# First feed-forward layer: one block normalized on GpSimd, second root and shared products reordered; token weights and the lines' bias moved

## The chip, the cores and the metric

The kernel runs on one core of a Trainium2 chip. The metric is the time of one execution on the device in microseconds (us); where several executions were timed, their median counts.

## The reference

`x` is (2, 2048, 256) in float32. Three layers follow one another, each added to `x`:

```python
x = x + 0.5 * ffn(layernorm(x))
x = x + attention(layernorm(x))      # causal, 16 heads, queries and keys are normalized line coordinates
x = x + 0.5 * ffn(layernorm(x))

def ffn(x):                          # 4096 tokens, 16 experts, each token goes to 2 of them
    scores = softmax(x @ gate_w.T)   # + gate_b; the 2 best of 4 groups, then the 2 best experts
    y = sum over the 2 experts of weight * (silu(x @ We1 + be1) * (x @ We3 + be3)) @ We2 + be2
    z = silu(x @ ws1 + bs1) * (x @ ws3 + bs3) @ ws2 + bs2      # shared experts, 256 wide
    return y + z
```

## The kernel before

Tokens stand in 32 tiles of 128, in 8 blocks of 4 tiles. Each engine has its own program, written out by hand; the order of the work is the order of the code, and semaphores are all that joins the engines. The change touches the first feed-forward layer (`ffn`) and the stage behind it (`lines`), which adds the experts' rows to `x` and makes queries, keys and values.

**The front of `ffn`, from 0 to about 36 us.** VectorE takes the statistics of the blocks as they arrive, and sums them up in two halves (blocks 0 to 3, blocks 4 to 7). For each half ScalarE takes the root (`take_root`, L572) and VectorE inverts it (L695). Then the blocks are normalized into `stage` (`normalize`: VectorE at L701 makes blocks 0 and 4 to 7, ScalarE at L588 blocks 1 to 3). TensorE turns each block (L451, 8 transposes into two of four banks, so that block n waits for the copies of block n - 2), and the turned blocks are copied to `xnt` (`keep_tiles`: ScalarE at L557 for blocks 0 to 5, VectorE at L707 for 6 and 7). Between them TensorE multiplies products nobody reads (`keep_busy`, L440). From each half of `xnt` come the logits (`logits_of`, L428), which ScalarE copies (`keep_logits`, L561) and TensorE turns back (`turn_logits`, L435). VectorE's `softmax` (L778 to L792) subtracts the maximum, waits for ScalarE's exponential (`take_exp`, L577; its table is loaded at the `hint` of L609) and finds the group scores.

**The middle, to about 103 us.** TensorE makes six shared up products (`shared_up`, L472) and down products (`shared_down`, L485), each in turn, and between them the small products of the routing. VectorE works through the routing, multiplies (`multiply`, L735) and adds (`add_shared`, L743). The last routing product is the inversion (L512), which waits for ScalarE's scaled marks (L582); from it VectorE makes `token_of` (L899), by which GpSimd gathers the rows of each expert tile (`bring`, L668). Behind `token_of` VectorE adds the last shared product and then computes the token weights (`weigh`, L828 to L830), which only the lines stage reads.

**The expert loop, to about 231 us**, has 79 turns: TensorE turns gathered rows (L525), multiplies up (L536) one turn later and down (L547) three turns later. ScalarE copies the up weights (L636) and the turned rows (L641) and gates (L648). VectorE copies the down weights (L914), multiplies (L927, `prod_done`) and adds the bias (L921). An up product waits for the `prod_done` of two turns before, since it shares two banks.

**The lines stage, to about 373 us.** For each block GpSimd gathers the experts' rows (L1363), VectorE adds them to `x` (`add_rows`, L1632), takes statistics (L190), subtracts (L1681 to L1684), and splits lines (`split_lines`, L1690 to L1705); ScalarE normalizes (L233), copies points and values (L1535, L1537) and stores features (L1525); TensorE turns the block (L1419), turns features (L1438) and projects (L1453 to L1456). Two shared products of `ffn` are left over for this stage; the last is added by `add_shared(1)` (L1593) at VectorE's step 2, and when that is done TensorE multiplies a bias (`project_bias`, L1403), which VectorE adds (L1628) at the end of its step 2.

The attention (to about 873 us) and the second feed-forward layer follow.

## Time and profile before

| | |
|---|---|
| runs | 1141.83, 1141.98 and 1144.21 us, median 1141.98 |
| profiled execution | 1139.9 us, of which the trace spans 1137.9 |
| mean granted clock of TensorE | 0.988 of full speed |
| busy, share of the span | TensorE 90%, ScalarE 76%, VectorE 58%, GpSimd 40% |

The profile's views used here: the timeline lists each engine's instructions by start, with the length, the operation (output <- input), how many are merged in the row, and in brackets the idle time before them and what ended it. The windows give each engine's busy time in a stretch and TensorE's granted clock there (1.00 is 2.4 GHz, 0.50 is 1.2 GHz). Starts of instructions that follow on their engine can lie before the end of the one before them, since they overlap by some 0.1 us.

### The profile page before, as it was taken

The numbers are of one execution on the slowest core, as the hardware profiler recorded it, in microseconds if no ns is written. First come the engines' busy times: TensorE is split into PE (matmuls) and PEld (weight loads), VectorE is DVE, ScalarE is ACT, GpSimd is POOL, SyncE is SP. The second block draws the span as 40 slices with busy tenths as digits, with TensorE's granted clock in tenths as the row PEclk, the third lists the DMA queues.
The fourth block names the chain that finished last, engine by engine and source line by source line (L and its number), as shares of the span: only waits on it lengthen the run. The fifth ranks groups of instructions, "written<-read, shape, count | busy, mean of one in ns | idle before, by whom it ended". The sixth has DMA issues, their size and how long they took to land.

```text
span 1137.9 us, 23905 instructions
## 1 busy us (share of the span) xinstructions
PE 1028.8 (90%) x7549; PEld 559.1 (49%) x7549; DVE 664.2 (58%) x1477; ACT 870.4 (76%) x1245; POOL 460.0 (40%) x671
## 2 busy tenths in 40 slices
PE   8998999989887788989899898989899999999995
PEld 4456999946554122222122222222223578999843
DVE  6898788768997422332134345356548686445655
ACT  4226777745887999999999999999998237777710
POOL 1003666457730424331221323431313345677755
PEclk9999999999999899999999999999999999999998
DMA  8911555545766221020201022120100965566655
GB/s 291 276 58 48 172 162 173 155 128 162 223 211 196 73 72 56 11 61 10 66 11 41 30 71 79 29 76 20 48 1 21 282 190 157 166 190 188 182 162 153
DMA packets 125717, 133.80 MB, mean 118 GB/s; under 512 B 13224, under 2 KB 111888, under 8 KB 125616
## 3 DMA queue, kind: packets, MB, share of 16 engines
q1 hardware_dynamic: 109056, 90.95, 25.2%
q0 software_dynamic: 14448, 39.47, 12.9%
q10 hardware_dynamic: 2112, 2.10, 0.6%
q8 instruction: 56, 0.92, 0.3%
q14 instruction: 45, 0.37, 0.1%
HBM read 80.43 MB, written 52.04 MB: 116 GB/s over the span
## 4 chain that ended last, share of the span: by engine, by line
PE 31%; ACT 24%; issue 14%; DVE 8%; POOL 2%; DVEq 1%; DMA 1%; ACTq 0%; POOLq 0%
ACT wide L2077 22%; PE banks L1961 6%; PE banks L2452 6%; PE banks L2377 5%; PE banks L2466 3%; PE banks L1935 2%; PE banks L2386 2%; PE banks L2440 1%; DVE x_res L1632 1%; POOL wide L2083 1%; PE banks L1453 1%; DVE wide L1681 1%; PE banks L1456 1%; PE banks L1975 1%; DVE attn_lines_parts L190 1%
## 5 line engine op out<-in xcount | busy, mean ns | idle before, releaser
L2077 ACT ACTIVATE wide<-banks 128x1536 f32<-128x1536 f32 (+1 forms) x384 | 491.7, 1479 | 5.4 <-PE banks L1935 3.8
L1961 PE MATMUL banks<-wide,attn_attend_v_now 128*32 128x512 f32 (+3 forms) x2560 | 287.7, 540 | 1.7 <-POOL wide L2083 1.6
L2083 POOL TENSOR_SCALAR_AFFINE_SELECT wide<-wide 128x256 f32<-128x256 f32 (+1 forms) x320 | 118.2, 398 | 382.8 <-ACT wide L2077 379.1
L1935 PE MATMUL banks<-attn_attend_q_now,attn_attend_k_now 32*128 32x512 f16 (+3 forms) x1280 | 150.5, 354 | 57.4 <-ACT wide L2077 54.3
L1935 PEld LDWEIGHTS banks<-attn_attend_q_now,attn_attend_k_now 32*128 32x128 f16 x1280 | 38.7, 91 | 291.9 <-ACT wide L2077 246.9
L668 POOL DMA_INDIRECT f_region<-xn_rows,f_token_of x79 | 78.3, 991 | 125.1 <-DVE f_token_of L899 82.4
L2128 DVE COPY sums<-banks 128x512 f32<-128x512 f32 x32 | 22.1, 691 | 163.3 <-PE banks L1961 163.3
L2452 PE MATMUL banks<-f_xnt 128*128 128x128 f32 x752 | 100.5, 277 | 3.8 <-DVE f_more L2678 2.9
L2452 PEld LDWEIGHTS banks<-f_xnt 128*128 128x128 f32 x752 | 91.3, 191 | 6.7 <-issue 5.8
L2565 POOL DMA_INDIRECT last_rows_in<-xn_rows,f_spare x72 | 68.8, 956 | 62.1 <-DVE f_stage L2626 24.4
L1961 PEld LDWEIGHTS banks<-wide,attn_attend_v_now 128*32 128x32 f32 x2560 | 56.3, 108 | 73.7 <-issue 71.8
L536 PE MATMUL banks<-f_region,wide 128*128 128x128 f32 x632 | 84.4, 277 | 0.6 <-DVE wide L927 0.6
L2535 ACT ACTIVATE f_xnt<-last_w_all 128x514 f32 x94 | 59.5, 632 | 33.1 <-issue 24.2
L2670 DVE TENSOR_TENSOR f_xnt<-banks,last_w_all 128x256 f32<-128x256 f32 x94 | 39.9, 425 | 65.9 <-PE banks L2466 54.7
L536 PEld LDWEIGHTS banks<-f_region,wide 128*128 128x128 f32 x632 | 76.7, 191 | 2.4 <-issue 1.3
L636 ACT ACTIVATE wide<-f_w_all 128x514 f32 x79 | 50.0, 632 | 30.9 <-issue 30.4
L2156 DVE TENSOR_TENSOR x_res<-banks,x_res 128x512 f32<-128x512 f32 x30 | 20.7, 691 | 89.6 <-PE banks L1975 89.6
L2466 PE MATMUL banks<-last_w_all,f_more 128*128 x188 | 58.1, 391 | 1.5 <-DVE f_more L2678 1.5
L914 DVE COPY wide<-f_w_all 128x512 f32 x79 | 38.8, 491 | 19.8 <-issue 19.1
L547 PE MATMUL banks<-wide 128*128 128x256 f32 x158 | 47.1, 381 | 0.4 <-DVE wide L927 0.4
L2549 ACT ACTIVATE f_xnt<-banks,f_xnt 128x128 f32<-128x128 f32 x94 | 34.5, 367 | 10.6 <-PE banks L2452 9.4
L1363 POOL DMA_INDIRECT f_region<-y_slots,attn_lines_rows_of x32 | 37.8, 1183 | 11.8 <-issue 8.5
(370 smaller groups left out, 1765.2 us busy)
## 6 DMA issues: line engine op xcount, KB each, us to landing
y_half<-f_xnt SPq DMA_DIRECT2D x94, 128.0 KB
y_slots<-wide SPq DMA_DIRECT2D x79, 128.0 KB, 1.7
attn_v<-f_more SPq DMA_DIRECT2D x32, 256.0 KB, 3.0
attn_attend_v_now<-attn_v SPq DMA_DIRECT2D x32, 256.0 KB, 3.2
x_res<-L_attn_x SPq DMA_DIRECT2D x8, 512.0 KB, 7.5
xn_rows<-f_w_all SPq DMA_DIRECT2D x8, 512.0 KB, 5.1
attn_q<-attn_lines_q_out SPq DMA_DIRECT2D x8, 512.0 KB, 3.4
attn_k<-attn_lines_k_out SPq DMA_DIRECT2D x8, 512.0 KB, 4.1
```

Source lines behind the costliest of these rows:

```text
L536: last = pe.matmul(bank[2 + m][:, f * P:(f + 1) * P], w_up[:, at, col_at:col_at + INTER], rows_t[:, m, c * P:(c + 1) * P], start=(c == 0), ...
L636: act.activation(w_up[:, j, :], w_all[:, bass.ds(expert, 1), 0:UP].rearrange("p o f -> p (o f)"), ACT.Copy).then_inc(sem.up_kept, 1)
L668: pool.indirect_dma_start(out=rows_in[:, n % ROUND, :], out_offset=None, in_=xn_rows, in_offset=bass.IndirectOffsetOnAxis(ap=token_of[:, n ...
L1935: last = pe.matmul(score[i % SLOTS][:, j, column:column + columns(u)], k_now[rows, kt * P:(kt + 1) * P], q_now[rows, qc * QW + c0:(qc + 1) ...
L1961: last = pe.matmul(out_bank[qc][rows, c0:QW], v_now[:, kt, rows], probs[:, place, column:column + columns(u)], start=(kt == 0), stop=(u == ...
L2077: act.activation(probs_flat[:, at:at + width_of[i]], score_flat[i % SLOTS][:, 0:width_of[i]], ACT.Exp, scale=SCALE).then_inc(sem.exp_done, 1)
L2083: pool.affine_select(out=part, in_=part, compare_op=ALU.is_ge, fill=0.0, base=0, pattern=[[0, part.shape[1]], [1, P]], channel_multiplier= ...
L2377: last = pe.matmul(bank[f][:, :], ws13[:, c, f * P:(f + 1) * P], xnt_of(i)[:, c, :], start=(c == 0), stop=(c == DC - 1))
L2452: last = pe.matmul(bank[2 + m][:, f * P:(f + 1) * P], w_up[:, at, col_at:col_at + INTER], rows_t[:, m, c * P:(c + 1) * P], start=(c == 0), ...
L2466: pe.matmul(bank[4 + m][:, 0:D], prod_t[:, at, :], w_all[:, bass.ds(expert, 1), UP:UP + D].rearrange("p o f -> p (o f)"), start=True, stop ...
L2535: act.activation(w_up[:, n % ROUND, :], w_all[:, bass.ds(expert, 1), 0:UP].rearrange("p o f -> p (o f)"), ACT.Copy).then_inc(sem.up_kept, 1)
L2565: pool.indirect_dma_start(out=rows_in(n), out_offset=None, in_=xn_rows, in_offset=bass.IndirectOffsetOnAxis(ap=s.token_of[:, place_of_turn ...
```

## The change

Five edits, all in the order of the code.

1. Front: GpSimd normalizes block 3 (`POOL_BLOCK`), which ScalarE did. ScalarE takes the second root ahead of `keep_tiles(1)`. ScalarE keeps the turned blocks 0 to 4, 6 and 7, VectorE only 5.
2. Front: the first logits come after TensorE has turned block 4, not 5, and are turned back after block 5, not 6. ScalarE's table hint comes before the first `keep_logits`, and the first exponential between the copies of blocks 6 and 7. VectorE's `softmax` is cut in `shift` and the rest. TensorE's filler matmuls are 48 and 10, where they were 42, 4 and 4.
3. The token weights are computed in two parts, one ahead of each of the last two sums (`weigh_pick`, `add_half`), on a semaphore of their own.
4. In the expert loop, turn 1 alone: the up product of tile 0 goes ahead of the turning of tile 1's rows.
5. In the lines stage `add_shared(1)` goes ahead of the second pair of sums of VectorE's step 2, and `project_bias` ahead of block 1's projection on TensorE.

```diff
-        ACT_BLOCKS, DVE_TURNED = (1, 2, 3), (BLOCKS - 2, BLOCKS - 1)
+        ACT_BLOCKS, POOL_BLOCK, DVE_BLOCKS = (1, 2), 3, (0, 4, 5, 6, 7)
+        ACT_TURNED, DVE_TURNED = (0, 1, 2, 3, 4, 6, 7), 5
...
+            elif n == POOL_BLOCK:
+                eng.wait_ge(sem.pool_staged, 1)
             else:
-                eng.wait_ge(sem.staged, sum(m not in ACT_BLOCKS for m in range(n)) + 1)
+                eng.wait_ge(sem.staged, DVE_BLOCKS.index(n) + 1)
+
+        def wait_turned_kept(eng, n):
+
+            if n == DVE_TURNED:
+                eng.wait_ge(sem.dve_xnt_ready, DC)
+            else:
+                eng.wait_ge(sem.xnt_ready, DC * (ACT_TURNED.index(n) + 1))
...
-            keep_busy(42)
+            keep_busy(48)
...
-                    pe.wait_ge(sem.xnt_ready, DC * (n - 1))
+                    wait_turned_kept(pe, n - 2)
...
-                if n in (1, 2):
-                    keep_busy(4)
-                if n == HALF + 1:
+                if n == 1:
+                    keep_busy(10)
+                if n == HALF:
                     pe.wait_ge(sem.gate_ready, 1)
                     logits_of(0)
-                if n == HALF + 2:
+                if n == HALF + 1:
                     turn_logits(0)
...
+                second = isinstance(n, int) and n == 1
+                if runs(n, 0) and not second:
+                    turn(n, j, r)
...
+                if second:
+                    turn(n, j, r)
...
             keep_tiles(0)
             normalize(2)
-            keep_tiles(1)
             take_root(1)
-            normalize(3)
-            keep_tiles(2)
-            keep_tiles(3)
-            keep_tiles(4)
-            keep_tiles(5)
+            for n in (1, 2, 3, 4):
+                keep_tiles(n)
+            act.activation(hint[:], s.root[:, 0:1], ACT.Exp)
             keep_logits(0)
-            act.activation(hint[:], s.root[:, 0:1], ACT.Exp)
+            keep_tiles(6)
             take_exp(0)
+            keep_tiles(7)
             keep_logits(1)
             take_exp(1)
...
+            pool.wait_ge(sem.rstd_ready, 1)
+            for t in range(POOL_BLOCK * BT, (POOL_BLOCK + 1) * BT):
+                last = pool.tensor_scalar(stage[:, POOL_BLOCK, t % BT, :], x[:, t, :], s.mean[:, t:t + 1], s.rstd[:, t:t + 1],
+                                          ALU.subtract, ALU.mult)
+            last.then_inc(sem.pool_staged, 1)
...
-            for i in DVE_TURNED:
-                keep_tiles(i)
+            keep_tiles(DVE_TURNED)
...
+            shift(0)
             softmax(0)
+            shift(1)
             softmax(1)
...
+            def weigh_pick(k, pick):
+                dve.tensor_tensor(work, pick, probs, ALU.mult).then_inc(sem.weighed, 1)
+                dve.wait_ge(sem.weighed, 2 * k + 1)
+                dve.tensor_reduce(weight[:, k, :], by_expert(work), AX, ALU.add).then_inc(sem.weighed, 1)
+                dve.wait_ge(sem.weighed, 2 * k + 2)
+
+            def halve_weights():
                 step(dve.tensor_scalar(weight[:].rearrange("p k t -> p (k t)"), weight[:].rearrange("p k t -> p (k t)"), 0.5, None, ALU.mult))
...
-            add_shared(5)
-            weigh()
+            weigh_pick(0, first)
+            add_half(5, 0)
+            weigh_pick(1, second)
+            add_half(5, 1)
+            halve_weights()
...
                 last.then_inc(sem.turned, 1)
+                if isinstance(n, int) and n == 1:
+                    project_bias()
             if has_block(n, 2):
...
                     pe.matmul(bank[2 + j], now(1), w_now[:, 1, :], start=False, stop=True).then_inc(sem.projected, 1)
                 if isinstance(n, int) and n == 0:
                     shared_down(1)
-                if isinstance(n, int) and n == 1:
-                    project_bias()
...
                 combine_pair(n, q, r, 0)
                 if n == 2:
                     measure_lines(n - 1, q)
+                    add_shared(1)
                 stats.sum_up(dve, n, q, combine_pair(n, q, r, 1))
...
-                if isinstance(n, int) and n == 2:
-                    add_shared(1)
```

In the copies of blocks (`wide<-banks`) the output is `xnt`; `f_w_all` holds `stage`; `f_region` at the exponential holds the logits. ScalarE in the front, from the copy of block 0, before:

```order
L557 ACTIVATE wide<-banks 128x512 x2
L588 ACTIVATE f_w_all<-x_res,f_gap,f_rstd 128x256 x4
L557 ACTIVATE wide<-banks 128x512 x2
L572 ACTIVATE f_root<-f_var 128x16
L588 ACTIVATE f_w_all<-x_res,f_gap,f_rstd 128x256 x4
L557 ACTIVATE wide<-banks 128x512 x8
L561 ACTIVATE f_logits_t<-banks 128x512
L609 ACT_TABLE_LOAD
L609 ACTIVATE f_hint<-f_root 128x1
L577 ACTIVATE f_region<-f_region 128x256
L561 ACTIVATE f_logits_t<-banks 128x512
```

and with the change:

```order
L573 ACTIVATE wide<-banks 128x512 x2
L604 ACTIVATE f_w_all<-x_res,f_gap,f_rstd 128x256 x4
L588 ACTIVATE f_root<-f_var 128x16
L573 ACTIVATE wide<-banks 128x512 x8
L620 ACT_TABLE_LOAD
L620 ACTIVATE f_hint<-f_root 128x1
L577 ACTIVATE f_logits_t<-banks 128x512
L573 ACTIVATE wide<-banks 128x512 x2
L593 ACTIVATE f_region<-f_region 128x256
L573 ACTIVATE wide<-banks 128x512 x2
L577 ACTIVATE f_logits_t<-banks 128x512
```

The second root (`f_root`) stands one copy sooner, four normalizations are gone, the table is loaded before the first copy of logits, and two more copies of blocks stand around the first exponential.

VectorE from `token_of` (`f_token_of`) to the first copy of down weights, before:

```order
L899 TENSOR_TENSOR f_token_of<-f_token_f,f_empty_f 128x80
L743 SCALAR_TENSOR_TENSOR x_res<-banks,x_res 128x512 x2
L828 TENSOR_TENSOR f_region<-f_region 128x512
L829 TENSOR_REDUCE weight<-f_region 128x32
L828 TENSOR_TENSOR f_region<-f_region 128x512
L829 TENSOR_REDUCE weight<-f_region 128x32
L830 TENSOR_SCALAR weight<-weight 128x64
L911 TENSOR_LOAD f_expert_of
L911 ISA x2
L914 ISA
L914 COPY wide<-f_w_all 128x512
```

and with the change:

```order
L927 TENSOR_TENSOR f_token_of<-f_token_f,f_empty_f 128x80
L852 TENSOR_TENSOR f_region<-f_region 128x512
L854 TENSOR_REDUCE weight<-f_region 128x32
L760 SCALAR_TENSOR_TENSOR x_res<-banks,x_res 128x512
L852 TENSOR_TENSOR f_region<-f_region 128x512
L854 TENSOR_REDUCE weight<-f_region 128x32
L760 SCALAR_TENSOR_TENSOR x_res<-banks,x_res 128x512
L858 TENSOR_SCALAR weight<-weight 128x64
L942 TENSOR_LOAD f_expert_of
L942 ISA x2
L945 ISA
L945 COPY wide<-f_w_all 128x512
```

The two sums (`x_res<-banks,x_res`) stood together ahead of the weights; each now has a product and a reduction ahead of it, and one small instruction is left behind them.

TensorE in the lines stage, before, from the last tile of block 1's projection to the turning of features (`f_xnt`):

```order
L1453 MATMUL banks<-attn_lines_w_now,attn_lines_xt 128x512
L1455 MATMUL banks<-attn_lines_w_prev,attn_lines_xt 128x128 x2
L1456 MATMUL banks<-attn_lines_w_now,attn_lines_xt 128x512
L1403 MATMUL banks<-attn_lines_w_o,attn_lines_b_v_wide 128x256 x2
L1419 MATMUL banks<-ident,f_stage 128x128 x8
L1438 MATMUL banks<-ident,f_xnt 128x128 x32
```

and with the change, from the last shared down product (`wide,heads`) to the first tile of block 1's projection:

```order
L1425 MATMUL banks<-wide,heads 128x256 x8
L1450 MATMUL banks<-ident,f_stage 128x128 x8
L1434 MATMUL banks<-attn_lines_w_o,attn_lines_b_v_wide 128x256 x2
L1486 MATMUL banks<-attn_lines_w_now,attn_lines_xt 128x512
L1488 MATMUL banks<-attn_lines_w_prev,attn_lines_xt 128x128 x2
L1489 MATMUL banks<-attn_lines_w_now,attn_lines_xt 128x512
```

The bias product (`b_v_wide`) stood behind the projection and ahead of the turning of block 2; it now stands between the turning of block 1 and block 1's projection.

## Rows read from the trace of the kernel before

**Rows 1.** windows: us from:to, length, PE, PEld, DVE, ACT, POOL busy, PEclk, DMA
```profile
36.00:97.00 61.00, 60.60 (x227) 35.11 (x225) 56.37 (x85) 25.17 (x76) 0.00 (x0) 1.00 0.45 136
113.00:228.00 115.00, 114.93 (x881) 106.13 (x880) 90.89 (x228) 86.93 (x220) 68.43 (x70) 1.00 0.55 166
280.00:352.00 72.00, 61.66 (x367) 40.01 (x365) 68.60 (x161) 60.51 (x120) 36.67 (x34) 0.95 0.68 207
```

**Rows 2.** timeline of TensorE: second logit product, first shared up product
```profile
32.58 1.92 PE L428 MATMUL banks<-wide,f_gate_t 128*32 128x512 f32 x16 [1.47 <-DVE wide L707]
...
35.71 1.88 PE L472 MATMUL banks<-wide 128*128 128x512 f32 x4
```

**Rows 3.** timeline of ScalarE in the front (start us, length, operation, idle before)
```profile
20.30 1.10 ACT L557 ACTIVATE wide<-banks 128x512 f32<-128x512 f32 x2
21.25 0.25 ACT L572 ACTIVATE f_root<-f_var 128x16 f32<-128x16 f32 x1
...
28.84 0.60 ACT L561 ACTIVATE f_logits_t<-banks 128x512 f32<-128x512 f32 x1 [0.80 <-PE banks L428]
29.46 1.28 ACT L609 ACT_TABLE_LOAD   x1
```

**Rows 4.** timeline of VectorE in the front
```profile
21.53 0.25 DVE L695 RECIPROCAL f_rstd<-f_root 128x16 f32<-128x16 f32 x1 [1.75 <-ACT f_root L572]
21.82 5.26 DVE L701 TENSOR_SCALAR f_w_all<-x_res,f_mean,f_rstd 128x256 f32<-128x256 f32 x16
29.84 2.60 DVE L707 COPY wide<-banks 128x512 f32<-128x512 f32 x4 [2.76 <-PE banks L451]
```

**Rows 5.** timeline of TensorE at the start of the expert loop
```profile
107.44 0.44 PE L525 MATMUL banks<-ident,f_region 128*128 128x128 f32 x2
108.44 1.13 PE L536 MATMUL banks<-f_region,wide 128*128 128x128 f32 x8 [0.56 <-DVE wide L927]
```

**Rows 6.** timelines of VectorE, ScalarE and GpSimd at the same place
```profile
105.59 0.20 DVE L830 TENSOR_SCALAR weight<-weight 128x64 f32<-128x64 f32 x1
106.84 0.43 DVE L914 COPY wide<-f_w_all 128x512 f32 x1 [1.06 <-issue]
105.99 0.37 ACT L648 ACTIVATE f_region<-banks,wide 128x128 f32<-128x128 f32 x1 [0.49 <-PE banks L536]
...
107.16 0.37 ACT L641 ACTIVATE f_region<-banks 128x256 f32<-128x256 f32 x1
104.51 1.14 POOL L668 DMA_INDIRECT f_region<-xn_rows,f_token_of  x1 [0.31 <-issue]
```

**Rows 7.** timeline of VectorE in the lines stage
```profile
269.66 1.40 DVE L1632 SCALAR_TENSOR_TENSOR x_res<-f_region,weight,x_res 128x256 f32<-128x256 f32 x3 [1.32 <-DMA f_region<-y_slots,slots]
...
273.65 1.28 DVE L1593 SCALAR_TENSOR_TENSOR x_res<-banks,x_res 128x512 f32<-128x512 f32 x2
...
279.90 0.42 DVE L1628 TENSOR_TENSOR attn_lines_b_o<-banks,attn_lines_b_o 128x256 f32<-128x256 f32 x1 [0.71 <-PE banks L1403]
```

**Rows 8.** timeline of TensorE in the lines stage
```profile
270.07 1.12 PE L1453 MATMUL banks<-attn_lines_w_now,attn_lines_xt 128*128 128x512 f32 x2 [1.51 <-ACT attn_lines_xt L1515]
...
278.83 1.03 PE L1403 MATMUL banks<-attn_lines_w_o,attn_lines_b_v_wide 128*128 128x256 f32 x4
```

**Rows 9.** timeline of GpSimd, its one elementwise instruction in the front
```profile
17.57 0.41 POOL L662 TENSOR_SCALAR f_bs<-f_bs 128x256 f32<-128x256 f32 x1
```

**Rows 10.** timeline of TensorE: first turning, and filler matmuls in that stretch
```profile
15.01 1.06 PE L451 MATMUL banks<-ident,f_w_all 128*128 128x128 f32 x8 [1.34 <-DVE f_w_all L701]
...
18.43 1.91 PE L440 MATMUL banks<-ones 128*128 128x512 bf16 x4
```

**Rows 11.** windows again, one stretch of the front
```profile
17.50:20.70 3.20, 3.07 (x11) 1.53 (x10) 2.18 (x11) 3.20 (x8) 0.48 (x2) 0.50 0.98 344
```

**Rows 12.** source line L668, GpSimd's row gathers: min/median/max ns
```profile
L668 POOL DMA_INDIRECT f_region<-xn_rows,f_token_of x79: 940/947/1298, 100.4 to 220.4; - x79
```

**Rows 13.** timeline of ScalarE in the lines stage
```profile
286.77 0.84 ACT L1549 ACTIVATE wide<-attn_lines_line 128x768 f32<-128x768 f32 x1 [0.65 <-DVE attn_lines_line L1684]
```

42 lines of the change are left out of this document (21 added, 21 removed).

## The prediction

> **What bounds the kernel now.** I read the busy times by stage first, then the timeline of each engine at the places that the change touches. From 36 to 97 us TensorE works 60.60 of 61 us, and in the expert loop, from 113 to 228 us, 114.93 of 115; in the lines stage from 280 to 352 us it is VectorE, 68.60 of 72 [rows 1]. So time can only be won ahead of these stretches, where TensorE or VectorE get to their unbroken work late, and each microsecond won there moves all that follows, since the later order is fixed.
>
> There are three such places. In the front, TensorE waits 1.47 us before the second logits, which start at 32.58, and starts the shared products at 35.71 [rows 2]; ahead of them ScalarE takes the second root at 21.25, behind a copy that began at 20.30 [rows 3], VectorE waits 1.75 us for that root, and its copies of the last two blocks wait until 29.84 [rows 4]. At the end of the middle part the inversion waits for ScalarE's marks; nothing in the change shortens that chain, which starts behind VectorE's `multiply` and so moves with TensorE's products. At the start of the loop the third up product (108.44) waits for VectorE [rows 5], which is busy with token weights to 105.79 and first copies at 106.84 [rows 6]. In the lines stage VectorE adds a shared product at 273.65, on its own path, and waits 0.71 us for the bias product [rows 7], which TensorE makes at 278.83 [rows 8].
>
> **The front: 1.4 us won.** The root moves from 21.25 to 20.30 (the place of the copy), so its reciprocal and VectorE's 16 normalizations come 0.95 us sooner; they take 5.26 us [rows 4] and end at 26.13 where it was 27.08. ScalarE loses one block of normalizations. From 20.4 it copies blocks 1 to 4 at 1.10 us each [rows 3]. Each turning needs some 1.1 us and waits for the copy of two blocks before, and block 4 is staged by 22.2, so I put the end of the four copies at 25.0. The table load of 1.28 us and the hint's 0.2 then end at 26.5. The first logits (1.92 us, as the second [rows 2]) can start at 23.8, when block 3 is kept, and are done before that; their copy of 0.60 us [rows 3] ends at 27.1, and TensorE turns them (0.6) to 27.7 and block 6 to 28.6. ScalarE copies block 6 to 29.7, takes the exponential (0.4) to 30.1, and copies block 7 to 31.15. VectorE's copy of block 5 (two of the four in 2.60 us [rows 4]) ends by 28.2 and its `shift` by 29.0, ahead of the exponential. So the second logits start at 31.15 where it was 32.58: 1.43 us sooner, and from there to the first shared product the order is what it was. VectorE's routing gets more than 2 us ahead by the cut `softmax`, but its first `multiply` reads the third and fourth up product, so it falls back to TensorE's lead. I take 1.4 us.
>
> What carries this: GpSimd must have block 3 staged by 21.6, when TensorE gets to it. It waits only for the first reciprocal, at 13.4. An instruction of its kind and width took 0.41 us [rows 9], four of them 1.6 us. At twice that they would still be done at 16.7, so this costs nothing on TensorE's path, and the iotas and the halving behind them, which nobody needs before 78 us, are only some 0.1 us later than they were. The store of block 3 on SP's queue stands behind block 2's and now finds it ready. The stores and the loads of experts' weights move up with the normalizations; they were landed 30 us before the loop.
>
> The fillers: six more of 0.21 us end at 14.95, just ahead of the first turning at 15.01, and cover the 1.34 us that TensorE idled there [rows 10]. From 17.5 to 20.7 the granted clock was 0.50, which is 1.2 GHz [rows 11], after TensorE had idled these 1.34 us and, behind the first turning, 0.6 for a load. I take it that with the 1.34 filled the clock stays at 2.4 GHz. Then the ten fillers take 2.1 us from 18.1 and end before block 2 is staged (20.4).
>
> **The start of the loop: 0.85 us won.** The weights are four instructions of 0.72 us and one of 0.2. Two go in the wait for the first sum, of which 0.86 us was idle, and two in the wait for the second, 1.03 us. VectorE is through at 104.0 where it was 105.79, both without the front's lead. Its copies then begin at 105.05 (1.06 us of issue [rows 6]). ScalarE's first gate comes at 105.99 [rows 6]. With turn 1 reordered the first up product starts at 104.4 instead of 104.9, and the row copy of tile 1 is later by as much, so the gate stays near 106.05. The first `prod_done` is then at 106.8 (it was 108.3), and the third up product is held by the turning at 107.44 [rows 5] and by ScalarE's row copy of 107.16 to 107.53 [rows 6]. It starts at 107.65, 0.8 us sooner. The row of the next tile was issued 1.44 us after the gather of 104.51 [rows 6], which landed 2.9 us after its issue (its turning is the one of 107.44), so it is there by 108.9, where TensorE turned it at 109.84. From then TensorE has no gap. I take 0.85; bounds: 0 (if rows land a gather's time later) and 1.0.
>
> At this place the Trainium skill speaks against the change (SBUF — State Buffer, section "SBUF: two separate sides"): a VectorE copy from SBUF to SBUF in its fast mode locks GpSimd out of writing gather descriptors, and VectorE's copies now lie over more of the first gathers. By it the win would be some 0.5, if a gather is late by the most that one exceeded the median by. The trace has 79 gathers at 0.947 us in the median and 1.298 at most [rows 12], nearly all beside such copies. So the sum keeps 0.85.
>
> **The lines stage: 1.5 us won.** `add_shared(1)` is 1.28 us [rows 7] and moves into a place where VectorE waited 1.32 us for gathered rows (269.66), so it is nearly free there; the splitting of lines starts 1.0 us sooner, since the size's root then ends it, not the sum. The bias product is done long before, so the 0.71 us are gone too: 1.7 us at VectorE. Against it: TensorE's bias product, 0.86 us to the next start, waits for the sum to end at 269.2, so the projection starts at 270.1 to 270.35 where it was 270.07 [rows 8]. Behind it ScalarE's copies and features would end at 286.2 to 286.5, and its squares, which waited 0.65 us for VectorE [rows 13], now start then, while VectorE wants them at 287.1. That takes back 0.1 to 0.3 us. Queries behind this wait on TensorE are the block's projection and all turnings, which is why it counts. GpSimd's gathers are not moved by it and keep 4 us of lead over the sums. I take 1.5; bounds 0.9 and 1.7.
>
> Everything else is moved without a cost: two semaphores more are cleared at the end of the layer, of some fifty.
>
> **Sum.** 1.4 + 0.85 + 1.5 = 3.75 us. The profiled execution took 1139.9 us, so the like of it would take 1136.15. The runs shown have a median of 1141.98, 2.1 us above it; the forecast is for such a median, 1138.2 us, 0.33% faster. A measurement of this kernel tells some 0.2% (2.3 us) from no change, so the forecast stands only 1.5 us beyond that.
>
> **Rivals.**
>
> *The clock falls all the same.* If TensorE runs at 1.2 GHz from 17.5, the ten fillers are slow: four took 1.91 us there [rows 10]. Ten reach to about 21.7, block 2 is turned 1.2 us late, and the front's 1.4 is 0.2. Or it falls before the second logits: TensorE then idles from 29.4 to 31.15 behind turnings alone, and a stretch of 3.2 us at half speed costs 1.6. Either way the win is 2.2 to 2.5, and the time 1139.6. For it: it fell once in the trace behind less idleness than 2 us. Against it: it did not fall behind the 1.47 us [rows 2]. 20%.
>
> *GpSimd holds VectorE up.* By the same section of the skill GpSimd and some VectorE instructions exclude one another for a whole instruction. As a mechanism of this kernel: the four normalizations on GpSimd, 1.6 us at 0.41 [rows 9], lie beside VectorE's of block 0 and its statistics. Should VectorE stop for them, the second root is 1.15 us late again, the win is 2.6, and the time 1139.4. Against it: GpSimd's instruction [rows 9] ran beside statistics that took no longer for it. 7%.
>
> *Won places are taken by what is next.* The loop's first rows land when they did relative to their turnings (loop 0), or ScalarE sets the lines stage (0.9), or both: 2.3 us won, 1139.7. 14%.
>
> *Slower.* A low clock that lasts. TensorE is without a gap from 35.7, so half of each microsecond at 0.50 there is lost. The trace's stretch of 3.2 us [rows 11] costs 1.6. From 7.5 us of it on, the 3.75 are used up; ten would give 1.25 us slower, with a measurement's scatter 1143 to 1145. Nothing in the trace shows one so long; 3%.
>
> **Numbers.** The forecast gets 56%. Faster by over 0.2% holds most of it and about half of the first three rivals, less what scatter takes: 0.64. Within 0.2%: 0.32. Slower: 0.04. The range goes from 1135.4 (4.6 us won, if all bounds are high, and 2 of scatter) to 1141.2 (the rivals at 2.2, with 1.4 of scatter).
>
> **What would show it.** The second root near 20.3 and second logits near 31.2; granted clock 1.00 from 17.5 to 20.7; the first shared product at 34.3, and token rows asked for at 99.0; VectorE's first down copy at 103.6 where it was 106.84, and turnings without a gap from the fifth, 2.25 us sooner than before; in the lines stage VectorE without a wait behind its step 2, and the first exponential of the attention at 370.9 where it was 374.6. Wrong would be: a granted clock of 0.50 anywhere from 17 to 36 us, a shared product that starts behind 35, or a gap of ScalarE or TensorE behind block 1's projection that VectorE waits for.

## The result, and the profile after

The changed kernel takes 1139.9 us in the median of 12 runs (1137.84 to 1142.43), the kernel before 1142.52 us in the median of 12 beside it (1141.33 to 1145.58). The ratio is 0.9974, with a 95% interval of 0.9963 to 0.9985: 0.26% or 3.0 us faster, where 3.75 us were forecast. The profiled execution of the changed kernel spans 1138.2 us, 0.3 us *more* than the one shown of the kernel before. So one execution hides what the medians show, and the first question is why. Among the runs of all kernels below, one took 3473.52 us (edit 5 alone); the median given there counts it, the ratio leaves it out.

The windows of the changed kernel, answering to [rows 1] and [rows 11]:

```profile
core 0: us, PE busy (x) PEld busy (x) DVE busy (x) ACT busy (x) POOL busy (x), PEclk, DMA share, GB/s
36.00:97.00 61.00, 59.76 (x240) 35.20 (x240) 56.18 (x85) 25.40 (x78) 0.00 (x0) 1.00 0.42 127
113.00:228.00 115.00, 115.00 (x880) 106.21 (x878) 90.37 (x228) 86.42 (x219) 67.72 (x69) 1.00 0.54 164
280.00:352.00 72.00, 60.15 (x375) 39.15 (x376) 68.36 (x159) 62.40 (x124) 34.66 (x32) 0.98 0.69 212
17.50:20.70 3.20, 2.99 (x18) 1.57 (x17) 2.71 (x13) 3.20 (x8) 2.23 (x6) 1.00 0.96 333
102.90:104.70 1.80, 1.78 (x8) 1.80 (x9) 0.85 (x2) 0.63 (x1) 1.43 (x2) 0.50 0.33 87
104.70:106.00 1.30, 1.16 (x7) 0.79 (x5) 0.00 (x0) 0.57 (x2) 0.84 (x2) 0.50 0.39 107
...
366.00:369.00 3.00, 3.00 (x31) 3.00 (x29) 1.16 (x2) 2.13 (x3) 0.00 (x0) 0.50 1.08 316
```

The same engines fill the same stretches. What differs is the clock column. The front's low stretch is gone (1.00 from 17.5 to 20.7, where [rows 11] have 0.50), and low stretches stand at the start of the expert loop and at the end of the lines stage. The kernel before has two of its own in the lines stage, from 297 to 301 and from 325 to 328 us (hence its 0.95 in the window from 280), the changed kernel one from 308 to 311.

**The front** came as forecast. TensorE's timeline in the changed kernel, and GpSimd's:

```profile
18.14 2.12 PE L450 MATMUL banks<-ones 128*128 128x512 bf16 x9
20.43 3.42 PE L461 MATMUL banks<-ident,f_w_all 128*128 128x128 f32 x24 [0.16 <-ACT f_w_all L604]
...
31.01 1.92 PE L438 MATMUL banks<-wide,f_gate_t 128*32 128x512 f32 x16 [1.58 <-ACT wide L573]
...
34.14 2.31 PE L482 MATMUL banks<-wide 128*128 128x512 f32 x5
```

```profile
13.45 5.04 POOL L671 TENSOR_SCALAR f_w_all<-x_res,f_mean,f_rstd 128x256 f32<-128x256 f32 x4 [9.33 <-DVE f_rstd L714]
...
19.33 0.40 POOL L681 TENSOR_SCALAR f_bs<-f_bs 128x256 f32<-128x256 f32 x1
```

The first shared product starts at 34.14 where [rows 2] have 35.71: 1.57 us won. GpSimd's four normalizations took 5.04 us, not 1.6.

**The start of the loop** gave nothing in this execution:

```profile
101.95 0.41 PE L534 MATMUL banks<-ident,f_region 128*128 128x128 f32 x2 [1.46 <-DMA f_region<-xn_rows,f_token_of]
102.92 2.04 PE L550 MATMUL banks<-f_region,wide 128*128 128x128 f32 x8 [0.57 <-ACT f_region L655]
104.76 1.06 PE L534 MATMUL banks<-ident,f_region 128*128 128x128 f32 x4
105.96 1.29 PE L550 MATMUL banks<-f_region,wide 128*128 128x128 f32 x8
107.08 0.38 PE L534 MATMUL banks<-ident,f_region 128*128 128x128 f32 x2
107.30 1.06 PE L550 MATMUL banks<-f_region,wide 128*128 128x128 f32 x8
108.19 0.60 PE L563 MATMUL banks<-wide 128*128 128x256 f32 x2
```

Rows were asked for 1.57 us sooner, and VectorE made its first down copy at 103.20 where [rows 6] have 106.84. But the first up product's eight matmuls take 2.04 us, not 1.06: TensorE runs at 1.2 GHz. The lead was 1.56 us at the inversion and is 1.21 at the loop's steady turnings (108.63, was 109.84).

**The lines stage** gave 1.34 us, and lost 2.0 at its end. VectorE in the changed kernel:

```profile
267.10 1.28 DVE L1624 SCALAR_TENSOR_TENSOR x_res<-banks,x_res 128x512 f32<-128x512 f32 x2
268.30 1.79 DVE L1662 SCALAR_TENSOR_TENSOR x_res<-f_region,weight,x_res 128x256 f32<-128x256 f32 x4
...
272.85 0.23 DVE L1720 TENSOR_SCALAR attn_lines_size<-attn_lines_size 128x128 f32<-128x128 f32 x1
...
356.80 0.95 DVE L1648 TENSOR_REDUCE attn_lines_size<-wide 128x128 f32<-128x768 f32 x1 [4.01 <-ACT wide L1580]
...
363.98 2.23 DVE L1711 TENSOR_TENSOR wide<-f_spare 128x768 f32<-128x768 f32 x3 [1.50 <-ACT f_spare L1566]
```

The four sums at 268.30 have no wait ahead of them, where [rows 7] have 1.32 us, and the splitting of lines starts at 272.85, 2.0 us sooner. VectorE led the kernel before by 1.29 us at the stage's start, by 2.63 at block 3's size (L1648, 286.16; was 288.79), and by 2.61 at 356.80. Then TensorE's turnings of features ran at 1.2 GHz (351.20, 32 of them in 2.85 us where such 32 take 1.96 at 2.4 GHz), VectorE waited for ScalarE at 363.98, 1.22 us ahead of before, and the attention's first exponential started at 374.01, only 0.60 us sooner than before. How much of this is the clock's, the other profiles tell. From the reduction answering to 356.80 to the first exponential lie 15.19 or 15.20 us in all seven profiles (on chips like this one) without a low stretch between 352 and 358 us, the kernel before among them. With one it is 16.76 and 16.78 us in two kernels below, and 17.21 here, where a second stretch lies over the next 32 turnings too (365.74, 3.55 us). So a low stretch there costs 1.6 to 2.0 us. The rest went mostly in the second layer's expert loop (0.24 us ahead at its first product, 0.59 behind at its last); the length of that loop differs by 1.5 us among five executions at a granted clock of 1.00, so nothing in the change is needed for it.

Two theories follow. *A*: each place gives what its rows show, and the sum is 3.75 us. *B*: the places give that only while TensorE's clock is up. Low stretches of some 3 us come up once or more in the parts where TensorE idles, and when the front's is gone, one comes up where TensorE is needed.

### The profile page after: what moved, and what is told of

Its sections match the earlier page's. It is cut to its first block, busy times and chain, and to the rows that moved or that the text cites. A ratio compares the mean times of both kernels' runs of the same rounds, so it can differ in the third digit from the quotient of the medians.

```text
span 1138.2 us, 23920 instructions
## 1 busy us (share of the span) xinstructions
PE 1032.4 (91%) x7554; PEld 562.4 (49%) x7557; DVE 662.9 (58%) x1475; ACT 870.1 (76%) x1243; POOL 464.7 (41%) x675
## 4 chain that ended last, share of the span: by engine, by line
PE 30%; ACT 24%; issue 14%; DVE 7%; POOL 3%; DVEq 1%; DMA 1%; ACTq 0%; POOLq 0%
ACT wide L2107 22%; PE banks L1991 6%; PE banks L2482 6%; PE banks L2407 5%; PE banks L2496 3%; PE banks L1965 2%; PE banks L2416 2%; POOL f_region L1394 1%; PE banks L2470 1%; POOL wide L2113 1%; DVE x_res L1662 1%; DVE wide L1711 1%; PE banks L2005 1%; PE banks L1486 1%; DVEq L2696 1%
## 5 line engine op out<-in xcount | busy, mean ns | idle before, releaser
L2186 DVE TENSOR_TENSOR x_res<-banks,x_res 128x512 f32<-128x512 f32 x30 | 20.7, 691 | 89.6 <-PE banks L2005 89.5
```

## The experiments

They ran on several chips. On one, the kernel before itself took 1227.95 us; it is treated by itself. Ratios are always to the kernel before on the same chip, as they were recorded; they differ from the quotient of the two medians by up to 0.1%. "Behind the inversion" is the time from the inversion's end to the first down product: 10.89 us in the kernel before, 11.23 in the changed one.

### The edits apart, on the slower chip

```diff
# front alone: edits 1 and 2
+        ACT_BLOCKS, POOL_BLOCK, DVE_BLOCKS = (1, 2), 3, (0, 4, 5, 6, 7)
...
# loop alone: edits 3 and 4
+            weigh_pick(0, first)
+            add_half(5, 0)
...
+                if second:
+                    turn(n, j, r)
...
# lines alone: edit 5
+                    add_shared(1)
...
+                if isinstance(n, int) and n == 1:
+                    project_bias()
```

> The kernel before with the front's edits alone (1 and 2). Theory A (each place gives what its own rows show, and the places add up): the first shared up product starts 1.5 us sooner (34.2 us), nothing else changes its length, and the median is 1.5 us below the kernel before (ratio 0.9987). Theory B (TensorE's clock takes part of it back): the front still gives 1.5 us at its own end, but a stretch of 3 us at a granted clock of 0.50, which the kernel before had inside the front, now stands at another place where TensorE is needed, and the median is only 0.5 us or less below. Sign of it: the lead at the first steady turning of the expert loop is under 1.2 us.

> The kernel before with edits 3 and 4 alone (token weights between the last sums; first up product ahead of the second turning). Theory A (the edit frees VectorE, and the gates were its customers): the third up product and the steady turnings start 0.85 us sooner (109.0 us for the fifth turning, was 109.84), the granted clock stays 1.00 from 102 to 107 us since the front has taken its low stretch already, and the median falls by 0.8 us. Theory B (the order of the edit itself makes TensorE idle 1.46 and 0.57 us in a row, and the clock falls behind that): 0.50 from about 104 us, the first up product takes 2.0 us instead of 1.06, and the steady turnings come no sooner than before: gain 0 or a loss of 0.3 us. Theory C (ScalarE's gate and row copies bound it at any clock): clock 1.00 and gain under 0.3 us.

> The kernel before with edit 5 alone (the shared sum and the bias product sooner in the lines stage). Theory A: VectorE leads by 1.3 us from block 3 on (first normalization of block 3 at 288.8 where it was 290.12), and the attention's first exponential starts 1.3 us sooner (373.3, was 374.61); median 1.3 us lower. Theory B (a low clock of TensorE at the end of the stage takes it back): the lead of 1.3 us holds to 356 us and is gone at the first exponential if the granted clock is 0.50 in the last turnings of features, and stays if it is 1.00 there. Theory C (at the end of the stage ScalarE or TensorE bound, so that VectorE's lead is lost at any clock): lead under 0.5 us at the first exponential with a granted clock of 1.00 from 350 to 371.

> The changed kernel without its edits 3 and 4: front and lines alone. If the loop's edits gave 0.85 us under the changed kernel, this is 0.8 us slower than it, 2.1 us faster than the kernel before. If they gave nothing because the clock fell at the start of the loop (theory B), this is as fast as the changed kernel: 2.7 to 3.0 us faster than before (ratio 0.9975), and the lead at the fifth turning is 1.5 us, where the changed kernel had 1.21.

Measured: front 1226.82 us (ratio 0.9981, 0.9962 to 1.0), loop 1228.21 (1.0004, 0.9989 to 1.0019), lines 1230.62 (1.0022, 1.0005 to 1.004), front with lines 1230.28 (1.0023, 1.0007 to 1.0038). The intervals of the first two are too wide for their forecasts of 0.13% and 0.07%: the medians settle neither. Up to the loop the profiles can be read like the others. The first shared product was 1.5 to 1.7 us sooner in both kernels that have its edits (34.27 and 34.33; 35.85 and 35.99 in the two that have not). At the loop's start, with edits 3 and 4 alone:

```profile
103.57 0.41 PE L524 MATMUL banks<-ident,f_region 128*128 128x128 f32 x2 [1.37 <-DMA f_region<-xn_rows,f_token_of]
104.54 1.13 PE L540 MATMUL banks<-f_region,wide 128*128 128x128 f32 x8 [0.57 <-ACT f_region L647]
...
108.66 0.60 PE L553 MATMUL banks<-wide 128*128 128x256 f32 x2
```

The first down product comes 10.00 us behind the inversion, against 10.88 in the kernel with edit 5 alone, whose loop is that of before. So edits 3 and 4 give 0.88 us up to this product at full clock, and theory C of that run (ScalarE bounds it) falls. What becomes of it behind this product can't be read here: all four kernels on this chip have a further wait of 1.4 to 1.8 us ahead of an up product between 111 and 114 us, with the edits and without. Theory B of the same run has this execution against it: TensorE idled 1.37 and 0.57 us, and the clock stayed. In both kernels with the front's edits it fell between 102 and 108 us, though their loop is that of before (11.02 and 11.21 us behind the inversion). So the low stretch doesn't need the loop's edits; in these four profiles it goes with the front's. With the old loop it cost only 0.14 and 0.33 us there. The lead that theory B of the front's run wanted gone was 1.58 us at the fifth turning (108.54, against 110.12 in the kernel with edit 5 alone). Whether the loop's edits pay within the changed kernel, the question of the fourth run, stays unanswered here, since the changed kernel itself did not run on this chip.

The expectation for edit 5 was wrong here: a loss of 0.2%, not a gain. On this chip every engine stood for some 16 us early in the lines stage (ScalarE 16.37 to 16.72 us, up to 276 to 279 us), so the gathered rows had long landed, and the wait that was to hide the shared sum was not there. The wait for the bias product was there: 2.23 and 2.99 us of VectorE without edit 5, none with it. But with edit 5, alone or with the front's, ScalarE waited for transfers behind that, which it did not without:

```profile
310.58 1.02 ACT L1542 ACTIVATE attn_lines_q_out<-banks 128x1024 f16<-128x1024 f16 x1 [2.20 <-DMA x_res<-L_attn_x]
312.09 1.02 ACT L1542 ACTIVATE attn_lines_q_out<-banks 128x1024 f16<-128x1024 f16 x1 [0.48 <-DMA x_res<-L_attn_x]
314.28 1.02 ACT L1542 ACTIVATE attn_lines_k_out<-banks 128x1024 f16<-128x1024 f16 x1 [1.17 <-DMA x_res<-L_attn_x]
317.14 1.02 ACT L1542 ACTIVATE attn_lines_k_out<-banks 128x1024 f16<-128x1024 f16 x1 [1.84 <-DMA x_res<-L_attn_x]
```

VectorE's step from block 2's reduction to block 3's takes 21.56 us in both kernels with edit 5, against 17.93 and 18.51 in the two without: the gain at the bias product is more than lost. Why transfers land later there, and why only with edit 5, stays open. All runs below are from chips on which the kernel before takes 1143 to 1144 us.

### The changed kernel again

Nothing is edited.

> The changed kernel again, as it is, as the level for the two kernels with fillers and as a second profile. On a chip like the first: 1139.9 us, ratio 0.9974 to the kernel before, first down product 11.2 us behind the inversion with the granted clock at 0.50 around 103 to 106 us. Theory B (the fall at the loop's start is a consequence of the front's edits and comes every time) wants the low stretch again; if it is a matter of the single execution, the clock is 1.00 there in this one.

Measured: 1141.13 us, ratio 0.9966 (0.9951 to 0.9982), which is 3.9 us by the ratio and 2.8 by the medians. Its twelve runs fall into two groups, four from 1136.57 to 1137.79 and eight from 1140.07 to 1143.36 us. The mean granted clock doesn't tell the groups apart (0.984 and 0.985 are in both). The profiled run is one of the four. Windows, then TensorE:

```profile
102.00:104.00 2.00, 1.39 (x11) 1.21 (x12) 0.68 (x3) 1.02 (x2) 1.70 (x2) 1.00 0.41 125
104.00:106.00 2.00, 1.78 (x15) 1.43 (x14) 0.95 (x3) 1.52 (x4) 1.39 (x3) 1.00 0.25 72
252.00:255.00 3.00, 2.00 (x3) 0.97 (x4) 1.92 (x6) 0.95 (x2) 2.39 (x3) 0.57 0.39 108
255.00:258.00 3.00, 3.00 (x14) 2.04 (x13) 2.45 (x10) 0.66 (x2) 2.22 (x3) 0.86 0.36 111
```

```profile
102.05 0.41 PE L534 MATMUL banks<-ident,f_region 128*128 128x128 f32 x2 [1.44 <-DMA f_region<-xn_rows,f_token_of]
103.02 1.13 PE L550 MATMUL banks<-f_region,wide 128*128 128x128 f32 x8 [0.56 <-ACT f_region L655]
...
107.09 0.60 PE L563 MATMUL banks<-wide 128*128 128x256 f32 x2
```

With the same waits of 1.44 and 0.56 us, the clock stays at 2.4 GHz here, and the first down product comes at 107.09, 10.01 us behind the inversion. The same program, 1.22 us apart at this place: whether the clock falls here is a matter of the single execution. Nor is there a low stretch from 352 to 356 us, and the first exponential comes at 371.98, 2.03 us sooner than in the first profile; their spans are 2.2 us apart. One came at 252 us, which the first profile hasn't, where VectorE then waited 2.27 us for ScalarE's root. The Trainium skill (TensorE: Matmul & The Clock Gate, "Part 1: The HAM clock gate") says of the slow matmuls at a kernel's start that their count differs between executions of the same kernel; the two traces show the like in the middle of one (0.50 and 1.00 in the same place).

### Fillers at the loop's start, and in the lines stage

`fill(k)` multiplies k products of 128x512 in bf16 that nobody reads, into a bank that is free then.

```diff
# loop: both kernels
+            fill(6)
...
+                    if second:
+                        fill(2)
...
# lines: the second kernel only
+                if after(n, 3):
+                    pe.wait_ge(sem.q_ready, 2 * (n - 2))
+                    for _ in range(8):
+                        pe.matmul(bank[6][:, :], core.ones[:], core.ones[:, 0:1].to_broadcast([P, BW]), start=True, stop=True)
```

> The changed kernel with eight filler matmuls more at the start of the expert loop: six while TensorE waits for the first gathered rows, two between the first turning and the first up product; into a bank that nobody reads then. The edits 3 and 4 without the front's gave 0.88 us there (first down product 10.00 us behind the inversion's end, against 10.88 in the kernel before), at a granted clock of 1.00; with the front's edits the clock fell at this place in every profile so far, and the first down product came 11.23 us behind the inversion in the changed kernel. Theory B (the low stretch of 3.2 us moved from the front to the loop's start and takes the gain of edits 3 and 4): with fillers the granted clock is 1.00 from 100 to 108 us, the first down product comes 10.0 to 10.1 us behind the inversion, and this kernel is 1.0 to 1.2 us faster than the changed one on the same chip, if the low stretch does not then come up at another place that counts. Theory D (the clock falls here whatever TensorE does): 0.50 all the same, and fillers delay the first up product by up to 0.4 us: 0 to 0.4 us slower.

> As the kernel with fillers at the loop's start, and in the lines stage eight filler matmuls (1.7 us) in TensorE's wait of 2.2 to 2.7 us ahead of each turning of features from block 1's on. Theory B: in the changed kernel VectorE's lead of 2.6 us over the kernel before fell to 0.6 us in the last 15 us of the stage, where the granted clock was 0.50 in 351 to 355 and 366 to 369 us. With fillers the clock is 1.00 there, and the attention's first exponential comes 1.5 to 2 us sooner than without. Theory C (ScalarE bounds the end of the stage): the clock is 1.00 and the first exponential comes no sooner, and the time is that of the kernel without these fillers. If a filler is in the way, VectorE's steps get longer than 14.1 us.

Measured: fillers at the loop 1139.05 us (ratio 0.9958, 0.9943 to 0.9972; 5 runs from 1137.97 to 1140.11), at both places 1137.95 us (0.9953, 0.9938 to 0.9968; 5 runs from 1136.71 to 1139.28), against 0.9966 without. Both had a granted clock of 1.00 to 250 us and the first down product at 107.09. None of the ten runs is above 1140.11 us, where seven of the twelve without fillers are. With the lines' fillers the clock was 1.00 to 369 us, and the first exponential came at 371.61, with the loop's alone at 372.26, where the two executions without fillers had 374.01 and 371.98. That is 0.65 us for the lines' fillers, not the 1.5 to 2 expected: the profile without them had no low stretch from 352 to 356 us either, so this pair can't show what they prevent. Theory D (the clock falls whatever TensorE does) has every profile with fillers at the loop's start against it, these two and three more below. The medians differ by less than their intervals; the places in the traces and the narrower spread carry the reading.

The gain at the first down product isn't kept whole where the rows come late. With fillers at both places the sixth turning waits for them:

```profile
109.66 0.44 PE L540 MATMUL banks<-ident,f_region 128*128 128x128 f32 x2 [0.34 <-DMA f_region<-xn_rows,f_token_of]
```

It stands 12.54 us behind the inversion, where the kernel with the loop's fillers alone and the changed kernel's second profile have 12.07 and 12.06, and the kernel before 12.87. So of 0.9 us at the first down product 0.3 to 0.8 are left one turn later.

### Fillers at three places

```diff
# as above, and behind the first turning of the lines stage
+                if isinstance(n, int) and n == 0:
+                    for _ in range(6):
+                        pe.matmul(bank[2][:, :], core.ones[:], core.ones[:, 0:1].to_broadcast([P, BW]), start=True, stop=True)
```

> The kernel with fillers at the loop's start and in the lines stage, and six more behind the first turning of the lines stage, where TensorE idles 1.51 us ahead of block 0's projection (the clock was 0.50 behind it, from 252 to 257 us, in two of four executions on such a chip). Theory B: granted clock of 1.00 from 0 to 365 us in every profile, VectorE's reduction of block 3 (286 us) no later, median 0.3 to 0.8 us below that of the kernel with fillers at two places (1137.95, ratio 0.9953): ratio 0.995. Rival (that place is off the path, VectorE bounds it): same time, ratio 0.9953.

Measured: 1137.15 us (1136.46 to 1137.89, 5 runs), ratio 0.9945 (0.9931 to 0.9958). Its windows, and the first exponential:

```profile
0.00:36.00 36.00, 29.78 (x169) 15.81 (x171) 26.00 (x86) 16.59 (x36) 9.51 (x32) 1.00 0.86 278
36.00:97.00 61.00, 59.75 (x239) 35.13 (x239) 56.19 (x84) 25.61 (x78) 0.00 (x0) 1.00 0.43 128
97.00:113.00 16.00, 15.39 (x102) 12.43 (x100) 11.28 (x29) 8.53 (x20) 10.93 (x11) 1.00 0.34 96
228.00:280.00 52.00, 47.68 (x190) 27.84 (x193) 40.62 (x96) 25.91 (x51) 35.54 (x37) 1.00 0.49 138
280.00:352.00 72.00, 67.58 (x416) 41.80 (x419) 68.19 (x156) 62.18 (x122) 37.30 (x32) 1.00 0.70 214
352.00:366.00 14.00, 12.33 (x71) 7.08 (x71) 8.27 (x13) 10.20 (x19) 0.00 (x0) 1.00 0.78 241
```

```profile
369.60 1.28 ACT L2122 ACT_TABLE_LOAD   x1
370.89 2.37 ACT L2122 ACTIVATE wide<-banks 128x1280 f32<-128x1280 f32 x2
```

With the clock at 1.00 all the way to 366 us the attention starts at 370.89, 3.72 us sooner than before: the place that the prediction gave as 370.9. The lead is 1.35 us at the inversion, 2.09 at block 0's projection (253.23, was 255.32) and 3.72 at the end of the stage, so the three places give 1.35, 0.74 and 1.63. This version beats the kernel before; its five runs also lie at the low end of the changed kernel's (five of whose 24 are as low). Against fillers at two places (0.9953) it can't be told.

### Edit 5 undone under a held clock

```diff
# the kernel with fillers at three places
-                    add_shared(1)
...
+                if isinstance(n, int) and n == 2:
+                    add_shared(1)
```

`project_bias` stands behind block 1's projection again, too.

> The kernel with fillers at three places, but without edit 5: the last shared sum and the bias product of the lines stage stand where they stood before. With the clock held, the places should add up as predicted: the front 1.4, the loop's start 0.85, the lines stage 1.5 us. Theory A under a held clock: VectorE's reduction of block 3 comes 1.3 us later than the 284.81 us of the kernel with edit 5, the attention's first exponential at 372.2 where that one had 370.89, and the median is 1.3 us higher, 1138.4 us on a like chip (ratio 0.9957, where that one had 0.9945). Rival (the lead of the lines stage is not kept through the attention): the same 1.3 us at the first exponential, and under 0.5 us in the median (ratio 0.9945 to 0.995).

Measured: 1138.9 us (1137.59 to 1140.96, 9 runs), ratio 0.9966 (0.9954 to 0.9977). Block 3's reduction came at 286.75 (with edit 5: 284.81), and the first exponential:

```profile
372.62 5.97 ACT L2123 ACTIVATE wide<-banks 128x1280 f32<-128x1280 f32 x5
```

That is 1.73 us later than 370.89, and the medians are 1.75 us apart (2.4 us by the ratios, the chips being different). The intervals of the two ratios still touch (from 0.9954 to 0.9958), so that edit 5 is worth its 1.5 to 2 us to the end, and that the attention doesn't swallow it, is likely rather than settled. What edit 5 saves here is one wait:

```profile
277.86 0.42 DVE L1674 TENSOR_TENSOR attn_lines_b_o<-banks,attn_lines_b_o 128x256 f32<-128x256 f32 x1 [1.91 <-PE banks L1442]
```

VectorE finds its gathered rows landed (four sums in a row at 265.82), so there is no wait in which to hide the shared sum. It waits 1.91 us for the bias product behind TensorE's projection instead, and block 3's reduction is 1.94 us later. With the front and the loop sooner, the bias product's place is the part of edit 5 that pays, not the sum's.

### Fillers without the change

```diff
# on the kernel before: six ahead of the first rows, two ahead of the second, eight a block in the lines stage
+            fill(6)
...
+                    if isinstance(n, int) and n == 1:
+                        fill(2)
```

> The kernel before, with no edit of the change, but with the fillers at the loop's start (six and two) and in the lines stage (eight a block). It tells what fillers are worth by themselves. Theory B: in the kernel before the low stretches fell on the front and on two places of the lines stage that VectorE covered, so fillers at these places buy little: 0 to 1 us (ratio 0.999 to 1.000), and nearly all of the 5 to 6 us of the kernels with edits and fillers needs both together. Rival (fillers alone do it, by keeping the clock up in the lines stage and the attention behind it): 2 to 3 us faster (ratio 0.998).

Measured: 1141.04 us, ratio 0.998 (0.9971 to 0.9989): 2.3 us faster. The rival's number was right, theory B's 0 to 1 us too low: fillers pay nearly as much without the change. The profile doesn't say from where: its first exponential is late (376.31; a low stretch from 255 to 259 us), so the gain in the median comes from other executions, or lies behind the lines stage. Between this kernel and the one with the change and three fillers lie 3.9 us of median (0.35% by the ratios). That is the change, one filler place more, and the low stretches that this kernel still has (17 to 20 and 255 to 259 us).

### The front's old fillers

```diff
-            keep_busy(48)
+            keep_busy(42)
...
-                if n == 1:
-                    keep_busy(10)
+                if n in (1, 2):
+                    keep_busy(4)
```

> The changed kernel with the fillers of the kernel before in the front (42, 4 and 4 in place of 48 and 10), all else as it is. Theory B (a low stretch of TensorE's clock comes once in this part, where TensorE idles, and the new fillers only moved it out of the front): 0.50 from 17 to 21 us again, first shared up product 0 to 1.3 us later than the changed kernel's 34.14 us, and then no low stretch at the loop's start, with the first down product 10.0 us behind the inversion's end. Median within 1 us of the changed kernel's and all runs in one group, where the changed kernel's twelve fell into two (1136.6 to 1137.8 and 1140.1 to 1143.4 us in the last series). Rival: the fillers matter only where they are: the front is 1.2 us longer, the loop's start is as uncertain as in the changed kernel, median 1.2 us slower.

Measured: 1140.99 us, ratio 0.9973 (0.9957 to 0.9988), as the changed kernel. The clock:

```profile
15.00:18.00 3.00, 2.21 (x18) 1.97 (x19) 3.00 (x10) 1.34 (x6) 3.00 (x3) 0.94 1.07 343
18.00:21.00 3.00, 2.67 (x9) 1.36 (x9) 2.27 (x11) 3.00 (x8) 1.72 (x6) 0.50 0.87 306
102.00:105.00 3.00, 1.73 (x12) 1.34 (x12) 1.57 (x5) 1.02 (x2) 2.09 (x4) 1.00 0.32 93
105.00:108.00 3.00, 2.77 (x23) 2.56 (x23) 1.37 (x5) 2.52 (x7) 2.39 (x3) 1.00 0.33 97
```

The low stretch is back in the front, the first shared product is 0.78 us later (34.92), and the loop's start is clean (10.02 us behind the inversion). So the front's new fillers gain 0.8 us there; the median shows nothing of it, which its interval of 1.8 us either way would allow in any case. The attention counts as well: this profile has low stretches at 430 to 434 and 690 to 693 us, and from the first exponential to the second layer's first gathered turning it takes 553.2 us, where the kernel before takes 550.8. With the old ones the clock fell in the front in all five profiles that have them, and never at the loop's start; with the new ones and none at the loop, it never fell in the front and fell at the loop's start in three of five. (With new ones in the front and fillers at the loop it fell in neither place, in four profiles.) That the front's fillers decide about the front is clear from this; that they move the low stretch to the loop rests on three of five against none of five, which is thin. That the runs would form one group was wrong: they go from 1138.34 to 1145.0, so the loop's start isn't the only place at which executions part.

### Block 3 on ScalarE

```diff
-            for t in range(POOL_BLOCK * BT, (POOL_BLOCK + 1) * BT):
...
             take_root(1)
+            normalize(3)
```

> The changed kernel with block 3 normalized by ScalarE behind the second root, not by GpSimd. ScalarE's four normalizations take 2.1 us, and all its copies stand behind them. If GpSimd's part is what carries the front, TensorE finds block 3 at 22.4 us instead of 21.5, ScalarE's four copies end at 27 us instead of 25, and the first shared up product starts at 35.5 to 36.2 us where the changed kernel has 34.14: 1.4 to 2.1 us slower, as slow as the kernel before. Rival (the sooner root alone carries it): first shared up product by 34.8 us, under 0.7 us slower.

Measured: 1142.67 us, ratio 0.999 (0.9977 to 1.0004), no longer told from the kernel before. TensorE waits for ScalarE's copies, and the first shared product is 2.15 us later than in the changed kernel:

```profile
23.96 2.04 PE L461 MATMUL banks<-ident,f_w_all 128*128 128x128 f32 x16 [2.02 <-ACT wide L573]
...
36.29 1.88 PE L482 MATMUL banks<-wide 128*128 128x512 f32 x4
```

GpSimd's block carries the front; the sooner root alone doesn't. This profile, too, has low stretches from 354 to 357, 432 to 436 and 692 to 695 us.

### Time and clock over all runs

Each run has its mean granted clock (the twelve of the kernel before beside the first result have none on record and are left out). On chips like the first, at 0.987 or more the kernel before has a median of 1141.2 us (6 runs) and the changed one 1137.8 (5 runs); at 0.984 to 0.986 they have 1143.6 (23) and 1139.9 (10); at 0.981 to 0.983, 1143.6 (18) and 1141.9 (9). So at a like clock the change is 3.3 to 3.7 us faster in the upper two classes and 1.8 in the third. At 0.980 or less only the kernel before was found (13 runs, 1145.7). This goes with theory B but doesn't prove it: the runs are from several chips, and the mean is over the whole kernel, not over the places that count.

## Why the prediction was right, and where it was wrong

- **The front, 1.4 us:** right by its own steps, 1.57 us. Root at 20.25 (20.3 forecast), four copies done at 24.97 (25.0), second logits at 31.01 (31.15), granted clock 1.00 from 17.5 to 20.7. One size was wrong in it: "an instruction of its kind and width took 0.41 us", four 1.6 us. They took 5.04 us, 1.26 each. They ended at 18.49 and were wanted at 21.5, so the slack carried the error, which was luck for this term. VectorE did not stop for them as the rival at 7% had it: its four normalizations beside them took 1.53 us, where they had taken 1.37. But the second half's variance was ready 0.34 us later, and 0.23 of it is one small instruction beside GpSimd's halving (19.33 to 19.73), which the four had pushed behind the statistics:

```profile
19.36 0.40 DVE L163 TENSOR_SCALAR f_mean<-f_mean 128x16 f32<-128x16 f32 x1
```

In the kernel before it took 0.17; it took 0.39 or 0.40 in all nine profiles with GpSimd's block, and 0.17 again in the one of the changed kernel with block 3 on ScalarE. So VectorE is held up beside GpSimd at one place, by a fifth of the rival's price of 1.15 us.

- **The start of the loop, 0.85 us:** right in size where the clock held: 0.88 us for edits 3 and 4 alone, and the same 10.0 us behind the inversion (9.92 to 10.02) in each of the eight profiles that have these edits and a clock of 1.00 there. In the changed kernel's first profile it was 1.22 us more, and the gain was gone. What the working left out is the clock: TensorE idles 1.46 and 0.57 us ahead of the first up product, and what it is granted behind that was not asked. "From then TensorE has no gap" was too strong as well: in three of the seven on chips like the first the sixth turning came 0.2 to 0.5 us later than in the others. The gathers themselves were no slower beside VectorE's copies (1.190 us at most, where 1.298 was the most before), so of the lock that the prediction weighed there is no sign here. The rival *The clock falls all the same* had the mechanism and, at 1.6 us, about the price, but put it in the front alone.
- **The lines stage, 1.5 us:** 1.34 us at block 3 in the first profile and 1.73 us when taken out under a held clock, around the 1.5 and within or just above the bounds. In the second case the split was another: all of it was the bias product's wait (1.91 us, forecast 0.71), and none the hidden sum. The step "the projection starts at 270.1 to 270.35 where it was 270.07" was too small: it started at 269.47 with a lead of 1.29 us, so 0.7 us late where up to 0.3 was worked out, but VectorE's steps didn't wait for it. Not foreseen was the end of the stage, where TensorE's turnings are on the path and a low stretch took 2 us of the lead.
- **The sum and the forecast:** the chance of 56% was for a kernel in which all three places pay. In the first profile the first exponential came at 374.01, not 370.9; in the second at 371.98; under fillers at 370.89. At a held clock the three places add up to 3.72 us, where 3.75 were forecast. The 3.0 us of the first series have an interval from 1.7 to 4.2, and the second series gave 3.9 by its ratio, so the medians alone neither show nor exclude a shortfall. That they mix executions with a low stretch at such a place and ones without is argued from two profiles, 2.2 us apart, and not shown run by run. In so far as the first median came out near the forecast although its profile lost 1.2 and 2.0 us to the clock, that was luck.
- **What the text gave as signs of error** (0.50 from 17 to 36 us, a late shared product, a gap behind block 1's projection) didn't occur; the low clock at 102.9 us was not on that list.
- **Two readings of the trace were wrong.** The clock "fell once in the trace", and "nothing in the trace shows one so long" as ten us: the kernel before was at 0.50 also at 298 and 326 us, and from 373 to 382 without a break. The long one begins where TensorE has nothing to do (until 376) and stands in both kernels alike, so it is no loss of the change; but low stretches outside the front were there to be seen.

On the slower chip the whole of edit 5 turned into a loss of 0.2%. No part of the prediction had a case for transfers that land later.

## What to carry to other kernels

Ahead of every place at which TensorE is about to be the bound, look at how long it idled and what the granted clock is there, and do so in several executions: behind an edit that fills one idle stretch the next may be the one that counts, and one profile shows only one of the outcomes. A few matmuls nobody reads, placed in the waits just ahead of those places, went with a steady gain here (five runs within 1.4 us of one another, where the changed kernel's twelve spread over 6.8) and were worth 2 to 3 us more; they were worth 2.3 us in the kernel before, too. Take the price of an instruction from a row with the same kinds of operands, not only the same width.

## What the runs showed that was not expected

- GpSimd's `tensor_scalar` on 128x256 in float32 took 1.26 us with a mean and a root per partition as its scalars (another input and output tile), and 0.40 with constants, in the same trace. Both kinds ran beside VectorE's statistics in one kernel or the other (0.41 at 17.57 us in the kernel before), so VectorE beside them is not the reason; no run separates the kind of scalar from the other tiles.
- Two executions of one program, with the same waits of 1.4 and 0.6 us, had granted clocks of 0.50 and 1.00 behind them.
- A filler of eight matmuls, 1.7 to 1.9 us at 2.4 GHz, in TensorE's wait ahead of each block's turnings of features cost next to nothing in VectorE's steps: the four from block 3's reduction on take 57.5 to 57.8 us with them and 57.4 to 57.9 without.
- Chips differ: the same kernel took 1142.5 to 1144 us in four series and 1228 in another.
